# Attention stage of a fused layer on eight cores: second x buffer, q/k block moved into the last chunk, scores and numerators round by round

## What is computed

```python
# x: (16, 2048, 1024) f32, 16 heads of 64
def attn(x):
    q, k, v = split(x @ W_attn + b_attn)           # to heads
    q = elu(q) + 1; k = elu(k) + 1
    # per head, causal scan over t:
    kv += k[t, :, None] * v[t, None, :]; ksum += k[t]
    y[t] = (q[t] @ kv) / (q[t] @ ksum + 1e-6)
    return y @ W_proj + b_proj
def ffn(x):
    h = gelu(x @ ternary(W_fc).T)                  # 4096 wide
    return layernorm(h, ln_w, ln_b) @ ternary(W_proj2).T
# ternary(W): sign(W) * min(round(|W| / (mean|W| + 1e-6)), 1)
x = layernorm(x + attn(x))
x = layernorm(x + ffn(x))
```

## Time and profile before

| | |
|---|---|
| time, two executions | 3473.83 and 3574.79 us, median 3524.31 |
| profiled execution | 3480.44 us; span of its slowest core 3478.9 us |
| spans of the eight cores | 3431.9 to 3478.9 us |
| granted TensorE clock, mean | 0.767 to 0.778 of full speed |
| busy | PE 59%, PEld (weight loads) 29%, DVE 24%, ACT 22%, POOL 6% |
| DMA | 237.47 MB, 68 GB/s on average |

### The profile page before, as it was taken

The page is one execution under the profiler, slowest core; times in us unless marked ns, Lnnn a source line. Parts: engine busy times, 40 slices in busy tenths (PEclk is TensorE's granted clock), DMA queues, the critical chain, the costliest instruction groups (busy, mean ns, idle before and its releaser), DMA issues.

```text
span 3478.9 us, 38486 instructions; the slowest of 8 cores (3431.9 to 3478.9 us)
## 1 busy us (share of the span) xinstructions
PE 2035.3 (59%) x12577; PEld 1026.0 (29%) x12746; DVE 824.1 (24%) x1789; ACT 780.6 (22%) x1695; POOL 222.7 (6%) x422
## 2 busy tenths in 40 slices
PE   0354553655536545553315322679797887979875
PEld 0132232332313323321212211234443433445342
DVE  2222221222213333432223222121112021120202
ACT  0233333433323222231113110102121211202120
POOL 0001011010110100101110111000000000000000
PEclk9966766767667667675657655989899999989997
DMA  4312123122231221211221222211203022130312
GB/s 128 102 46 88 49 79 103 40 79 64 79 100 44 73 70 40 79 61 52 70 70 40 70 70 76 67 43 49 95 15 109 31 80 67 43 104 7 109 43 97
DMA packets 108790, 237.47 MB, mean 68 GB/s; under 512 B 16434, under 2 KB 24626, under 8 KB 108596
## 3 DMA queue, kind: packets, MB, share of 16 engines
q1 hardware_dynamic: 83508, 167.86, 16.4%
q0 software_dynamic: 25088, 67.14, 4.9%
HBM read 167.82 MB, written 67.11 MB: 68 GB/s over the span
## 4 chain that ended last, share of the span: by engine, by line
PE 44%; DMA 24%; DVE 11%; ACT 10%; issue 9%; POOL 1%; DVEq 1%; SPq 1%; ACTq 0%; POOLq 0%
PE ps_qk L360 7%; DMA arena_f<-wpft 6%; PE ps_qk L818 6%; PE ps_wide L818 6%; PE ps_c L899 5%; PE ps_d L899 5%; DMA arena_f<-wfct 5%; PE ps_wide L551 5%; DMA out<-arena_f 4%; DMA arena_f<-x_fm 3%; DMA arena_b<-wqp_s 2%; PE ps L835 2%; DMA arena_f<-wattn 2%; ACT arena_b L491 2%; DVE arena_b L670 2%
## 5 line engine op out<-in xcount | busy, mean ns | idle before, releaser
L360 PE MATMUL ps_qk<-arena_b 128*128 128x512 bf16 x1001 | 246.3, 398 | 345.3 <-DVE arena_b L345 341.6
L899 PE MATMUL ps_c<-arena_b 128*128 128x512 bf16 x1000 | 238.1, 396 | 120.8 <-DVE arena_f L908 118.5
L360 PEld LDWEIGHTS ps_qk<-arena_b 128*128 128x128 bf16 x1024 | 96.2, 101 | 493.6 <-issue 408.9
L818 PE MATMUL ps_qk<-arena_b 128*128 128x512 bf16 x1001 | 233.6, 381 | 1.5 <-issue 0.3
L818 PE MATMUL ps_wide<-arena_b 128*128 128x512 bf16 x1006 | 232.0, 379 | 0.9
L899 PE MATMUL ps_d<-arena_b 128*128 128x512 bf16 x1000 | 225.3, 379 | 1.3
L551 PE MATMUL ps_wide<-arena_b 128*128 128x512 bf16 x480 | 167.5, 509 | 62.4 <-ACT arena_b L540 62.4
L446 PE MATMUL ps_c<-arena_b 64*128 64x128 bf16 x256 | 27.2, 232 | 301.2 <-DVE arena_b L453 301.2
L899 PEld LDWEIGHTS ps_c<-arena_b 128*128 128x128 bf16 x1024 | 101.1, 101 | 249.2 <-issue 144.8
L491 ACT ACTIVATE arena_b<-ps_c,arena_f 128x64 bf16<-128x64 f32 x256 | 59.5, 316 | 480.8 <-DVE arena_f L485 480.8
L591 PE MATMUL ps_c<-arena_f 128*128 128x128 f32 x128 | 34.8, 427 | 199.2 <-ACT arena_f L579 180.2
(11 more groups left out here) (145 smaller groups left out, 2853.8 us busy)
## 6 DMA issues: line engine op xcount, KB each, us to landing
arena_f<-wfct SPq DMA_DIRECT2D x128, 256.0 KB, 3.3
arena_f<-wpft SPq DMA_DIRECT2D x128, 256.0 KB, 3.1
arena_f<-x_fm SPq DMA_DIRECT2D x64, 256.0 KB, 3.3
arena_f<-x_tm SPq DMA_DIRECT2D x32, 512.0 KB, 4.6
x2tm_s<-arena_f POOLq DMA_DIRECT2D x32, 512.0 KB, 3.8
arena_f<-x2tm_s SPq DMA_DIRECT2D x32, 512.0 KB, 3.4
t_s<-arena_f POOLq DMA_DIRECT2D x32, 512.0 KB, 2.9
arena_f<-t_s SPq DMA_DIRECT2D x32, 512.0 KB, 4.4
```

Source lines behind the costliest of these rows:

```text
L360: ins = e.matmul(pq[:, 0:512], b(FULL, WQK_O + k * 2048 + m * 128, 128), b(FULL, XFM_O + k * 512, 512), start=(k == 0), stop=(k == KC - 1))
L818: ins = e.matmul(psh, AB[:, WQFC_O + k * 4096 + hc_ * 128: WQFC_O + k * 4096 + (hc_ + 1) * 128], b(FULL, X2FMBB_O + k * 512, 512), start=( ...
L899: e.matmul(psr[:, 0:512], AB[:, HFM_O + hc_ * 512 + c * 128: HFM_O + hc_ * 512 + (c + 1) * 128], b(FULL, WQPT_O + hc_ * 1024 + half * 512, ...
```

## The change

Three things are done, and the memory for them is rearranged.
1. `xfm` has two sets of eight tiles. `load_xfm(sc + 1)` is recorded at the start of stage `sc`, and `qk_mms(sc + 1)` is recorded inside the last chunk of stage `sc`, between the kv update and the transposes of y.
2. Numerators of a round are recorded directly behind the scores and the mask of the same round. The masked scores have two tiles in place of four.
3. Both groups of x2 transposes go to the bank `ps_7`.

The rows for the biases of v and of the projection and the row `UROW` lie at the same offset on the partitions 0, 32 and 64, and there are rows of ones on the partitions 32 and 64 too.

```diff
-        xfm = [B_(f"xfm{k}") for k in range(KC)]
+        xfm = [[B_(f"xfm{bi}_{k}") for k in range(KC)] for bi in range(2)]
...
         def load_xfm(sc, dep_ops=()):
             seq, t0 = sc // 4, (sc % 4) * SCT
+            bi = sc % 2
...
-        at = [B_(f"at{r}") for r in range(4)]
+        at = [B_("ath0"), B_("ath1"), B_("ath0"), B_("ath1")]
...
-        def chunk_attn(cg):
+        def chunk_attn(cg, filler=None):
...
+                    P.add("vector", lambda e, r=r, psr=psr:
+                          e.tensor_tensor(out=b(FULL, AT_O + (r % 2) * 512, 512), in0=psr[:, 0:512],
                                           in1=b(FULL, MASK4B_O, 512), op=OP.mult),
                           reads=[pbr, mask4], writes=[at[r]])
-
-            if ON('num'):
-                for r in range(4):
...
+                    if ON('num'):
+                        psr, pbr = (ps_c, pc) if r % 2 == 0 else (ps_d, pd)
...
+            if filler is not None:
+                filler()
+
             if ON('yt'):
...
                 for r in range(2):
-                    psr, pbr = (ps_c, pc) if r == 0 else (ps_d, pd)
-                    def x2t(e, r=r, psr=psr):
+                    def x2t(e, r=r):
...
-                    P.add("tensor", x2t, reads=[x2tm, identf], writes=[pbr])
...
+                    P.add("tensor", x2t, reads=[x2tm, identf], writes=[p7])
...
         for sc in range(n_sc):
-            if ON('qk'):
-                qk_mms(sc)
+            if sc == 0 and ON('qk'):
+                qk_mms(0)
+            if sc + 1 < n_sc:
+                load_xfm(sc + 1)
             for c in range(CPS):
                 cg = sc * CPS + c
-                chunk_attn(cg)
+                filler = None
+                if c == 3 and sc + 1 < n_sc and ON('qk'):
+                    filler = (lambda s=sc: qk_mms(s + 1))
+                chunk_attn(cg, filler=filler)
                 if ON('tasks'):
                     a_tasks_for_chunk(cg)
-            if sc + 1 < n_sc:
-                load_xfm(sc + 1)
```

More of the change, by code:

```diff
@@ L151, in build_core_program @@
         WQFC_O = 0
[L152 to L159, removed]
+        ROWP_O = 32768
+        BVROW_O = ROWP_O
+        BPROW_O = ROWP_O
+        UROW_O = ROWP_O
+        CROW_O = 33792
+        ONEROW_O = 34816
+        IDENTB_O = 34944
+        ONECOL_O = 35072
+        A0 = 35088
         WQK_O = A0
@@ L208, in build_core_program @@
         XFMSTG_O = AF0
-        XTM_O = AF0 + 512
+        XFMSTG2_O = AF0 + 512
+        XTM_O = AF0 + 1024
         X2TM_O = XTM_O + 1024
@@ L364, in qk_mms @@
                 hmm = P.add("tensor", mmfn,
-                            reads=[wqk[k] for k in range(KC)] + [xfm[k] for k in range(KC)],
+                            reads=[wqk[k] for k in range(KC)] + [xfm[bi][k] for k in range(KC)],
                             writes=[pqb])
@@ L428, in vfn @@
                                         b((0, 1), BVROW_O + half * 512, 512), start=False, stop=True)
-                    P.add("tensor", vfn, reads=[xfm[k] for k in range(KC)] + [wv[k] for k in range(KC)]
-                          + [rows, ones], writes=[pb])
+                    P.add("tensor", vfn, reads=[xfm[sc % 2][k] for k in range(KC)]
+                          + [wv[k] for k in range(KC)] + [rows, ones], writes=[pb])
                     P.add("vector", lambda e, half=half, psh=psh:
@@ new lines, in chunk_attn, with numfn, ysc @@
+                    if ON('num'):
+                        psr, pbr = (ps_c, pc) if r % 2 == 0 else (ps_d, pd)
+                        def numfn(e, r=r, psr=psr, c=c, kvbr_o=kvbr_o):
+                            for j in range(4):
+                                h = heads_round[r][j]
+                                fch, half = h // 2, h % 2
+                                atsl = b(FULL, AT_O + (r % 2) * 512 + j * 128, 128)
+                                qsl = AB[64 * half:64 * half + 64,
+                                         QFM_O + fch * 512 + c * 128: QFM_O + fch * 512 + (c + 1) * 128]
+                                kvo = kvbr_o + (h // 2) * 65
+                                kv_num = AB[64 * half:64 * half + 64, kvo:kvo + 64]
+                                kv_ks = AB[64 * half:64 * half + 64, kvo + 64:kvo + 65]
+                                e.matmul(psr[:, j * 65:j * 65 + 64], atsl, b(FULL, VTM_O + h * 64, 64),
+                                         start=(j == 0), stop=False)
+                                e.matmul(psr[:, j * 65 + 64:j * 65 + 65], atsl, b(FULL, ONECOL_O, 1),
+                                         start=False, stop=False)
+                                e.matmul(psr[:, j * 65:j * 65 + 64], qsl, kv_num, start=False, stop=False)
+                                ins = e.matmul(psr[:, j * 65 + 64:j * 65 + 65], qsl, kv_ks,
+                                               start=False, stop=(j == 3))
+                            return ins
+                        P.add("tensor", numfn, reads=[at[r], vtm, ones, kvbr] + [qfm[m] for m in range(8)],
+                              writes=[pbr])
+                        P.add("vector", lambda e, r=r, psr=psr:
+                              e.tensor_scalar(out=f(FULL, DSTG_O, 4),
+                                              in0=psr[:, 64:64 + 3 * 65 + 1:65],
+                                              scalar1=MIX_EPS, scalar2=None, op0=OP.add),
+                              reads=[pbr], writes=[stats])
+                        P.add("vector", lambda e, r=r: e.reciprocal(out=f(FULL, RECS_O + 4 * r, 4),
+                                                                    in_=f(FULL, DSTG_O, 4)),
+                              reads=[stats], writes=[recs])
+                        def ysc(e, r=r, psr=psr):
+                            for j in range(4):
+                                h = heads_round[r][j]
+                                ins = e.activation(out=b(FULL, YTM_O + h * 64, 64),
+                                                   in_=psr[:, j * 65:j * 65 + 64], func=AF.Copy,
+                                                   bias=0.0, scale=f(FULL, RECS_O + 4 * r + j, 1))
+                            return ins
+                        P.add("scalar", ysc, reads=[pbr, recs], writes=[ytm])
```

79 lines of the change are left out of this document (41 added, 38 removed).

## The result

The changed kernel takes 3517.72 us, the kernel before 3486.45 us beside it; the ratio is 1.0105, with an interval of 1.0079 to 1.013. So it is slower by about 36 us, half of the 70 us of the forecast, and within 2%: inside the forecast's wide range, and just under its narrow one of 3520 to 3580. (The 3524 us of the first timing of before come from one ordinary execution and one that was disturbed as a whole, and the ratio leaves such executions out.)

What follows compares the result with a forecast made beforehand. The attention phase was taken as bound by a chain hopping between engines, none full. From 3480 us, 66 gained, 93 and 43 lost, and 0 for the rest gave 3550 us, range 3465 to 3605.

Steps and rivals of the forecast that it cites:

- Part 1: Stage starts, second x buffer and early q/k: 60 us gained over seven, 13.8 at the last, 7.5 lost at chunk 0.
- what is hidden is only what TensorE does meanwhile: Stage starts: casts stay late, the wait moves to the next first mask; only k transposes and v matmuls are hidden.
- The 1.2 us of the projection: Projection behind the early q/k block: its matmuls run faster, 4.2 us against 5.39 busy, gaining 1.2 us per stage start.
- The first rival: Stage starts: casts find data early, all seven waits (199 us) vanish, extra costs stay; 3417 us, chance 0.07.
- Part 2: Scores and numerators round by round: rounds of 3.0 us lose 2.5, 3.1 or 3.2 us per chunk, 93 us in all.
- both distances to scaling 3: From mask 0, 12.1 us against 9.6 before; from bank c free behind weight sums, 6.8 us against 3.6.
- The second rival: Numerator rounds cost nothing because TensorE waits for ScalarE anyway in stages 0 to 3; 3457 us, chance 0.16 including times between.
- Part 3: Both groups of x2 transposes in one bank: second copy late and the delay passed on in 24 chunks, 43 us lost.
- 1.8 us late: Second x2 copy: its transposes wait for the first copy, and it follows 1.62 us after their start.
- 16 chunks, 29 us: Stages 0 to 3: weight sums stand behind the x2 copies on ScalarE, so the whole delay is passed on.
- Eight chunks, 14 us: Stages 6 and 7: quantizing on VectorE waits for the copies through POOL's stores and the single staging tile.
- The third rival: Projection and v matmuls: short waits keep TensorE's clock low, about 1.3 us more per chunk; about 3590 us, chance 0.17.

Runs made afterwards that it cites:

- e3: Changed kernel with round-by-round numerators and the one-bank x2 transposes both undone, leaving the second x buffer and early q/k block; 3415.56 us, 0.9808 of the kernel before.
- e2: Changed kernel with only the x2 transposes put back into two banks, ps_c and ps_d; 3486.11 us, ratio 1.0021 to the kernel before.
- e1: Changed kernel with only the numerators put back behind all scores and masks; 3423.87 us, ratio 0.9845 to the kernel before.
- e4: e3 with two x_fm loads per chunk recorded ahead of its weight slices and their casts one chunk later; ratio 0.9556 to the kernel before.
- e9b: Kernel before with only its x2 transposes moved to ps_7, timed again with more executions; 3491.78 us, ratio 1.004 to the kernel before.

## Why the forecast was right in its mechanisms and double in size

I compare TensorE's k transposes of chunk 0 and of chunk 31 on core 0. Between them lie 1868.0 us before, 1895.8 in the changed kernel, 1792.8 in e3, 1873.0 in e2 and 1808.7 in e1. Of the 30 us by which core 0's span grows, 28 lie in these 31 chunks. Single cores scatter: core 4 has 1877.4 before and 1899.2 in the changed kernel.

**Part 1, forecast 66 us gained, measured 67 (e3).** That the two agree within 1 us is luck, as the interval is 13 us either way. The step "what is hidden is only what TensorE does meanwhile" held. The 1.2 us of the projection are there as well: behind q/k of stage 1 its 18 matmuls are at full clock and busy for 4.35 us, in the stretch

```profile
375.00:380.00 5.00, 4.35 (x18) 1.59 (x18) 0.33 (x1) 0.00 (x0) 0.00 (x0) 1.00 0.01 3
```

where the earlier trace rows have 5.39 us at 0.71. Chunk 0 waits 14.3 us from its k transposes to its first mask, not 5.6: 8.7 us where I had 7.5. The first rival asked for the time of a fully hidden load. The rule it leans on (the Trainium skill, Trainium Kernel Development and Optimization, Best Practices, on double-buffering) names the right tool, but the buffer alone gave 67 of the 199 us; e4 shows that the place of the loads in the two queues gives the next 88.

**Part 2, forecast 93 us lost, measured 74 to 90.** The length of a round, 3.0 us, and both distances to scaling 3 came out within 0.1 us. Between e3 and e2 the chunk times grow by 22 us in the eight first chunks, 35 in the twelve behind weight sums, 23 in the eleven others with quantizing (core 0): 80 (76 on core 4), where the forecast has 91 for these 31. The second rival, that it costs nothing, falls.

**Part 3, forecast 43 us lost, measured 14 (e9b), 13 (e1 against e3) and 29 (e2). This is the step that failed**: "1.8 us late", passed on whole in "16 chunks, 29 us" and "Eight chunks, 14 us". Three things were mis-sized. The delay itself was 1.4 us between the copies. The transposes began 0.2 us earlier, so that the second copy, counted from the start of the last instruction of the statistics (L575, in the changed kernel L583), went from 4.3 to 5.45 us, 1.2 late. And not all of it was passed on: the sums and the quantizing wait for loads in between, and these absorb a part. With e3 and e1, which differ in part 3 alone, the last weight sum comes 0.8 us later (counted from there, 19.3 and 20.0 us on core 0, 19.5 and 20.3 on core 4, means of 12 chunks). In stages 6 and 7 of the changed kernel the second write on DVE, after chunk 25, is this:

```profile
1689.13 0.75 DVE L677 SCALAR_TENSOR_TENSOR arena_b<-arena_f,arena_b 128x512 bf16<-128x512 f32 x1 [7.87 <-DMA wqp_s<-arena_b]
...
1717.75 0.75 DVE L677 SCALAR_TENSOR_TENSOR arena_b<-arena_f,arena_b 128x512 bf16<-128x512 f32 x1 [1.64 <-DMA wqp_s<-arena_b]
1719.82 0.68 DVE L459 TENSOR_TENSOR arena_b<-ps_c,arena_b 128x512 bf16<-128x512 f32 x1
```

The chain through POOL is there (7.87 us of idle, 6.63 before) and that write comes 12.9 instead of 11.7 us after the same point, the full 1.2 us. But in the chunks 25 to 29 the eighth write and the mask come at 41 to 42 and 43 to 44 us in both kernels, only about 0.5 us later in the changed one. Between the second write and the eighth stand waits for the loads of the slices, and from write to write the delay shrinks.

**The third rival**, the clock, did not come: the projections of 31 chunks take 189.4 us on core 0 and 182.4 on core 4, where they take 196.9 and 183.3 before. Between e3 and e2, which differ in part 2 alone, they go from 179.8 to 179.5 us and from 187.8 to 191.3, where this rival asked for some 40 us. The clock was low around the projection in the kernel before already (0.71 and 0.58 in the earlier trace rows), and part 2's extra waits did not lower it further. The rule behind this rival (the Trainium skill, TensorE: Matmul & The Clock Gate, A second HAM failure mode: psum-queue depth-cycling) is of short idles between groups of matmuls that make the clock go up and down; no run here shows that more of them cost more.

Of the 34 us between forecast and result, part 3 explains 14 to 30 us and part 2 the rest, depending on which pair of runs one takes.

## What to carry to other kernels

A second buffer moves a wait only as far as the queues allow: look where the load stands in the issuing queue and where its consumer stands on its engine, and move these too (67 us became 155 here, and 175 with `gamma_fin` moved too). Do not split a pipelined group of small matmuls into rounds that wait for another engine, when two banks let one round's work cover the other's mask. And a delay at the head of a chain that waits for several loads need not arrive at its length: 1.2 us arrived as 0.5 to 0.8 here. Read how much of an earlier change at that place reached the end, or put a lower bound of zero on it.

## What had not been expected

The order in which an instruction's semaphore waits are issued matters. The recording layer issues one wait per semaphore. In e3 the first x2 transpose has three, and the one that comes last in time, ScalarE's, is issued first; the two others stand behind it though they were satisfied long before, and the trace shows 0.36 us from ScalarE's end to the start instead of 0.14. That the waits behind it are what takes the 0.22 us is the reading that fits, as only their order differs. Reversing the order on all engines took 2.1% off e3 with the work unchanged; the x2 transposes' own 0.22 us make only 7 of these 73 us. That each late wait costs the same was not measured, nor which of the waits makes most of the 73 us. It also fits the x2 transposes of the changed kernel, which begin 0.2 us earlier (449.83-449.69 = 0.14 us after ScalarE's end in chunk 4): they wait for one semaphore in place of three.
